# Second half of the node counts moved from the build into pass 0 of a two-network GNN kernel

## The chip, the cores and the metric

The kernel runs on one core of one Trainium2 chip. The metric is the device time of one execution in microseconds (us), as the median of several runs; less is faster. The kernel before takes 1076.45 us (median of 3 runs, 1075.31 to 1078.13). A core has four engines that compute (PE, the matrix engine; DVE, the vector engine; ACT, the scalar engine; POOL, the general one) and SP, which here only issues DMA transfers and waits. POOL issues DMA transfers too. Engines wait for each other and for transfers by semaphores: an instruction waits until a counter has reached a value.

## The reference: what is computed

A graph of 6250 nodes (64 features each) and 200000 directed edges (src to dst, sorted by dst, 16 attributes each) goes through two small networks, each followed by a residual sum and a layer norm:

```
def sage_conv(x, src, dst, W_l, b_l, W_r, n_nodes):        # first network, two of these
    msg = x[src]
    agg = segment_sum(msg, dst)
    cnt = segment_sum(ones, dst)
    mean = agg / maximum(cnt, 1.0)
    return mean @ W_l.T + b_l + x @ W_r.T

def mp_layer(x, src_f, dst_f, ea_f, W, b):                 # second network, three of these
    m = concatenate([x[dst_f], x[src_f], ea_f], axis=1) @ W.T + b
    return relu(segment_sum(m, dst_f))                     # with a self loop on each node

x = layernorm(x + conv2(relu(conv1(x))))
x = layernorm(x + mp3(bn_relu(mp2(bn_relu(mp1(x))))))
```

The change concerns `cnt` of the first network: how many edges end in each node, and 1 / max(cnt, 1), by which the sum over a node's neighbours is divided.

## The kernel before, in words

The kernel never gathers messages. In a first part, `build`, it makes the dense matrix of edge multiplicities (6272 by 6272, one byte each, `adj` in DRAM) in 25 stages of 256 columns. Each of the five aggregations (passes 0 to 4) is then a matrix product of the node features (`Xop`) with `adj`, in 13 blocks of 512 columns (`NB`), 49 matmuls of 128 rows to a block.

In the build DVE makes one-hot tables and unpacks finished stages (`unpack`, L806 and L807), PE multiplies tables (L929), ACT evacuates. POOL writes each unpacked stage to `adj` (`keep`, L631). Because all of pass 0 needs only the input features, its products are made in the build: of the first 21 stages by `product` (L904), stored in DRAM as `s0`, and of the last four by `remaining` (L314), which leaves its result in PSUM. Stages 21, 22 and 23 are multiplied at the end of the build and stage 24 behind the barrier, at the start of pass 0. Two staging buffers (`Xop1` and a part of `Aring`) take turns: stage 24 is unpacked into the one that stage 22 was in, so its unpack waits on `s_fin` for the product of stage 22.

The build also sums the edge attributes of each node (`ea_sum`, 33 rows in DRAM; row 32 is the count). The counts become factors in two pieces: nodes 0 to 3583 (`EARLY`) within the build, and nodes 3584 to 6271 (the later nodes) at its end. For a piece SP loads row 32 of `ea_sum` as 16 partitions (L599), DVE runs `counts` (sum for a check, max with 1, reciprocal, scale: L1090, L1092, L1094, L1096), and SP stores the result in `rc_d` (L604). From `rc_d` SP broadcasts the factors to 128 partitions (`reciprocals`, L299), in three pieces: blocks 0 and 1, blocks 2 to 5, blocks 6 to 12. Only the third needs the later nodes' counts of `rc_d`. `products` (L292) brings `s0` back in four pieces, and `given` (L305) brings the transposed input features `in_xT` in two, the second of 1312 KB after the last unpack, since it overwrites what the unpack reads (`F`).

What SP issues, it issues in the order of its program, and all of it goes through one queue. A barrier over all engines stands between the build and pass 0 (L379), and another between passes (L1162).

Pass 0, for each block b: DVE multiplies the stored product by the factors (`sums`, L1832, two instructions), PE applies two weight matrices (`post`, L1659 and L1660), ACT the relu (L2011), PE the next layer's weights (`post2`, L1687), DVE updates the residual and splits the result into a high and a low half (`rest`, L1901, L1891, L1893, L1894). DVE's program runs by turns: turn i holds `sums(i-1)` and then `rest(i-3)`. PE's turn i holds `post(i-1)` and then `post2(i-2)`. SP meanwhile waits for the later nodes' store and for the last writes of `adj` to land, and then loads the third piece of factors, the factors of pass 1, and the first six stages of `adj` (`Ares`, L1540). Passes 1 to 4 are dominated by the products (L1460).

Of the kernel before, what the change touches and what calls it, by code (L numbers as in the profile page):

```python
# [9 lines left out]
NP = NT * 128  # L10
SW = 256
NST = 25
# [106 lines left out]
NH = -(-NS // HS)  # L119
# [112 lines left out]
EARLY = 3584  # L232
# [38 lines left out]
def spread(m, name, cnt, a, b):  # L271

    x = (m["ea_sum"][32, :] if name == "ea_sum" else m[name])[a:b]
    return x.rearrange("(p c) -> p c", p=16), cnt[:, 0:(b - a) // 16]
# [10 lines left out]
def products(sp, m, i):  # L285

    b0, b1 = SUMS[i]
    stored = [st for st in range(2 * b0, min(NST, 2 * b1)) if RANK[st] < EARLIER]
    for z in range(2):
        sp.wait_ge(m["s_so"][z], 16 * max(RANK[st] // 2 + 1 for st in stored if RANK[st] % 2 == z))  # L290
    for c0, c1 in joined(stored):
        sp.dma_start(raw_sums(m)[:, c0:c1], m["s0"][:, c0:c1]).then_inc(m["s_sr"][i], 16)  # L292
# [84 lines left out]
def build(nc, ins, m):  # L377
    ctx = ExitStack()
    with ctx:  # L379
# [67 lines left out]
        ja = within(3, [128, RW], f16)  # L447

        late = G[0:16, 0, 0:(NP - EARLY) // 16].bitcast(f32)
        packed = m["F"][:].bitcast(u16).rearrange("p (r c) -> p r c", r=4)  # L450
        stage = [m["Xop"][1][:].rearrange("p a b -> p (a b)").bitcast(u16), m["Aring"][:, 1, 1, :].bitcast(u16)]

# [39 lines left out]
        s_st, s_eo, s_so = m["s_st"], m["s_eo"], m["s_so"]  # L492
# [25 lines left out]
        def unpacked_after(h):  # L518

            return [f for f in range(NST) if (stage_end[f] == h - 1 if h < NH else stage_end[f] >= h - 1)]  # L520
# [21 lines left out]
        def _(sp):  # L542
# [24 lines left out]
            for c in range(NCH):  # L567
# [6 lines left out]
                if c == NCH - 2:  # L574
                    for i in range(2):
                        sp.wait_ge(s_eo[i], 16 * (EARLY // SW // 2))
                    there, here = spread(m, "ea_sum", cnt, 0, EARLY)
# [7 lines left out]
            there, here = spread(m, "rc_d", cnt, 0, EARLY)  # L585
# [7 lines left out]
            given(sp, ins, m, 0)  # L593
            reciprocals(sp, m, 1)
            products(sp, m, 1)
            for i in range(2):
                sp.wait_ge(s_eo[i], 16 * (13 - i))
            there, here = spread(m, "ea_sum", late, EARLY, NP)
            sp.dma_start(here, there).then_inc(m["s_cl"], 16)  # L599
            products(sp, m, 2)  # L600
            products(sp, m, 3)
            sp.wait_ge(m["s_cr"], 8)
            there, here = spread(m, "rc_d", late, EARLY, NP)
            sp.dma_start(there, here).then_inc(m["s_cd"], 16)  # L604
            sp.wait_ge(s_un, NST)
            given(sp, ins, m, 1)

# [86 lines left out]
        def _(v):  # L694
# [170 lines left out]
            for i in range(3):  # L865
                nc.vector.tensor_scalar(m["ws"][i][:], m["ws"][i][:], m["scl"][:, 0:1], None, ALU.mult)
                nc.vector.tensor_scalar(m["wc"][i][:], m["wc"][i][:], m["scl"][0:97, 1:2], None, ALU.mult)
            for f in unpacked_after(NH)[:-1]:
                unpack(f)
            v.wait_ge(m["s_cl"], 32)  # L870
            counts(nc, v, late, m["csum"][:, 1, :], m["s_cr"], 4)
            unpack(NST - 1)

        @block.tensor
        def _(pe):
# [212 lines left out]
def counts(nc, v, cnt, total, s_cr, made):  # L1088

    nc.vector.tensor_reduce(total, cnt.rearrange("p (c i) -> p i c", i=4), AX.X, ALU.add).then_inc(s_cr, 1)  # L1090
    v.wait_ge(s_cr, made + 1)
    nc.vector.tensor_single_scalar(cnt, cnt, 1.0, ALU.max).then_inc(s_cr, 1)  # L1092
    v.wait_ge(s_cr, made + 2)
    nc.vector.reciprocal(cnt, cnt).then_inc(s_cr, 1)  # L1094
    v.wait_ge(s_cr, made + 3)
    nc.vector.tensor_single_scalar(cnt, cnt, 1 / CS, ALU.mult).then_inc(s_cr, 1)  # L1096
# [368 lines left out]
def propagate(nc, ins, m, t, p, sem, out, past, block, closing=None):  # L1465
# [30 lines left out]
    fused = p == 0 and not slow  # L1496
# [11 lines left out]
    @block.sync  # L1508
    def _(sp):
        def factors(b):  # L1510

            n, c = blk(b), b * 512
            if b >= 2:
                sp.wait_ge(s_r, b - 1)
            src = (m["rc_d"] if p <= 1 else m["ea_sum"][32, :])[c:c + n].rearrange("(o n) -> o n", o=1)
            rows = 128 if p <= 1 else 64
            sp.dma_start(rc[0:rows, b % 2, 0:n], src.broadcast_to([rows, n])).then_inc(s_c[b % 2], 16)

        def next_factors(b):

            src = m["rc_d"][b * 512:(b + 1) * 512].rearrange("(o n) -> o n", o=1)
            sp.dma_start(rc[:, b], src.broadcast_to([128, 512])).then_inc(t["s_cf"][b], 16)

        def late_factors():
            sp.wait_ge(t["s_cr"], 4)
            there, here = spread(m, "rc_d", t["cnt"], 0, NP)
            sp.dma_start(there, here).then_inc(t["s_cd"], 16)
            sp.wait_ge(t["s_cd"], 16)

        if fused:  # L1530
            sp.wait_ge(m["s_cd"], 32)
            for i in range(2):
                sp.wait_ge(m["s_st"][i], 16 * (13 - i))
            sp.wait_ge(m["s_fin"], NST - 1 - EARLIER)
            reciprocals(sp, m, 2)
            for b in range(2):
                next_factors(b)
            for b in range(RB):
                for h in range(2):
                    sp.dma_start(t["Ares"][:, b, h, :], m["adj"][2 * b + h]).then_inc(m["s_res"][b], 16)  # L1540
            sp.dma_start(F[64:97, 0:NP], m["ea_sum"][:, 0:NP]).then_inc(t["s_ea"], 16)
            sp.wait_ge(s_r, NB)
            for b in range(2):
                for h in range(2):
                    sp.dma_start(t["Aring"][:, b, h, :],
                                 m["adj"][2 * (RB + b) + h]).then_inc(t["s_ar"][b][h], 16)
            return
        if p == 0:
            late_factors()
        if p != 1 or slow:  # L1550
            factors(0)
            factors(1)
        for b in range(NB):
            nxt = b + 2 if b + 2 < NB else b + 2 - (NB - RB)
            if b >= RB and not slow and not (b + 2 >= NB and p == 4):
                i = ring(b)[0]
                sp.wait_ge(t["s_mm"], mm0 + b + 1)
                if (p, b) in CHECKED:
                    sp.wait_ge(t["s_ck"], CHECKED.index((p, b)) + 1)
                for h in range(2 if nxt < NB - 1 else 1):  # L1560
                    n = stage_width(2 * nxt + h)
                    sp.dma_start(t["Aring"][:, i, h, 0:NT * n], m["adj"][2 * nxt + h, :, 0:NT * n]).then_inc(
                        t["s_ar"][i][h], 16)
            if b + 2 < NB:
                factors(b + 2)
        if closing:
            closing(sp, lambda part, engine: part.run_sync(engine), lambda: None)
# [177 lines left out]
    def _(v):  # L1745
# [184 lines left out]
        if p == 0 and slow:  # L1930
            late_counts()

        lag = {1: 1, 4: 3}.get(p, 2)

        def turn(i):

            if (p, i) == (2, NB - 1):
                check(i)
            if 1 <= i <= NB:
                sums(i - 1)  # L1940
            if i >= lag + 1:
                rest(i - lag - 1)
            if (p, i) == (3, 2):
                check(1)
            if i < NB and (p, i) not in ((2, NB - 1), (3, 1)):
                check(i)
            if p == 4 and not slow:
                tell(i)
# [229 lines left out]
```

## Time and profile before

| what | before |
|---|---|
| median of 3 runs | 1076.45 us (1075.31 to 1078.13) |
| the profiled execution | 1076.73 us, of which the span of its instructions is 1074.9 us |
| granted TensorE clock, mean | 0.949 of full speed |
| PE busy | 925.9 us (86%) |
| DVE busy | 689.6 us (64%) |
| end of the build's last matmul, start of the next one | 398.81 us, 407.26 us |

The span counts from the first instruction to the last; the execution's own time lies 1.8 us above it. A row of the timeline gives the start, the time taken, engine, line, operation, output and inputs, how many instructions are merged in the row (x2), and in brackets how long the engine had been idle before and what ended that. Rows of SPq and POOL's DMA rows show the issue of a transfer, not the transfer. Matmul ends are modelled, so rows of PE overlap a little.

### The profile page before, as it was taken

What the parts mean: (1) busy time and instruction counts of PE and PEld (TensorE: products, weight loads), DVE (VectorE), ACT (ScalarE), POOL (GpSimd) and SP (SyncE); (2) the same over time, 40 slices, a digit from 0 to 9 for tenths busy, and PEclk for the clock granted to TensorE, in tenths of its full rate; (3) what the DMA queues carried; (4) which work ended last, traced back from release to release, by engine and by line L of the source; (5) the groups of instructions that cost most, each with busy time, mean ns of one, the idle gap of its engine ahead of it and who ended that gap; (6) DMA issues with size and microseconds to landing.
All of it is one profiled execution on the core that took longest, in us unless ns stands there. A gap on an engine that the chain in (4) does not pass through costs nothing. (4 is left out here: it accounts for less than half of the span.)

```text
span 1074.9 us, 19163 instructions
## 1 busy us (share of the span) xinstructions
PE 925.9 (86%) x7566; PEld 566.6 (53%) x7566; DVE 689.6 (64%) x1289; ACT 404.6 (38%) x846; POOL 129.8 (12%) x148
## 2 busy tenths in 40 slices
PE   0348877979687878999999999997999997999995
PEld 0347776868687864545555544444444444444443
DVE  5997989999999954623433656655385456332334
ACT  1684788889787821100000010104311022411113
POOL 4121323244322220000000000000000000000001
PEclk9868998989899998999999999998999998999998
DMA  6425546756576497953775607776018775037771
GB/s 176 82 77 204 189 134 203 254 143 211 176 213 185 110 339 255 370 230 140 295 311 204 250 16 291 309 271 251 21 32 320 295 280 240 11 106 296 269 282 31
DMA packets 64873, 217.02 MB, mean 202 GB/s; under 512 B 28955, under 2 KB 42860, under 8 KB 51236
## 3 DMA queue, kind: packets, MB, share of 16 engines
q1 hardware_dynamic: 55444, 164.26, 42.9%
q0 software_dynamic: 9328, 51.44, 13.7%
q8 instruction: 62, 1.02, 0.4%
q14 instruction: 39, 0.31, 0.1%
HBM read 170.43 MB, written 45.22 MB: 201 GB/s over the span
## 5 line engine op out<-in xcount | busy, mean ns | idle before, releaser
L1460 PE MATMUL PM<-Aring,Xop 128*128 128x512 fp8e4 (+1 forms) x1960 | 396.7, 363 | 2.0 <-issue 2.0
L1460 PEld LDWEIGHTS PM<-Aring,Xop 128*128 128x128 f16 x1960 | 182.2, 98 | 213.8 <-issue 11.0
L1460 PE MATMUL PM<-Ares,Xop 128*128 128x512 fp8e4 x588 | 137.1, 388 | 2.9 <-ACT Xop L2072 1.4
L929 PE MATMUL PM<-Aring 128*128 128x104 fp8e4 (+3 forms) x1616 | 96.8, 219 | 38.1 <-ACT F L998 38.1
L1834 DVE TENSOR_SCALAR S<-PM 128x256 f32<-128x256 f32 x72 | 30.5, 424 | 152.9 <-PE PM L1460 64.6
L2023 ACT ACTIVATE F<-PH,bag 64x512 f32<-64x512 f32 (+1 forms) x39 | 25.7, 660 | 260.5 <-PE PH L1677 259.9
L929 PEld LDWEIGHTS PM<-Aring 128*128 128x128 fp8e4 x1616 | 87.6, 105 | 41.4 <-ACT F L998 40.2
L1460 PEld LDWEIGHTS PM<-Ares,Xop 128*128 128x128 f16 x588 | 56.2, 100 | 70.5 <-issue 7.7
L1590 POOL DMA_DIRECT2D out<-hT x12 | 9.0, 754 | 654.0 <-DVE hT L1791 654.0
L782 DVE TENSOR_TENSOR Aring<-Ares 128x4096 uint16<-128x4096 uint16 x31 | 70.8, 2283 | 5.5 <-PE PW L929 5.2
L998 ACT ACTIVATE F<-PM 128x392 uint16<-128x392 f32 x147 | 67.2, 515 | 7.3 <-PE PM L929 5.7
L1864 DVE TENSOR_TENSOR hT<-hT,Aring 128x1536 uint16<-128x1536 uint16 (+2 forms) x71 | 67.6, 952 | 2.3
L789 DVE TENSOR_TENSOR Aring<-Ares 128x1144 uint16<-128x1144 uint16 (+22 forms) x139 | 67.2, 546 | 0.0
L904 PE MATMUL PX<-Aring,Xop 128*128 128x256 fp8e4 x490 | 58.5, 282 | 5.4 <-ACT Ares L1017 5.4
L904 PE MATMUL PX<-Xop 128*128 128x256 fp8e4 (+1 forms) x539 | 59.1, 271 | 0.6 <-ACT Ares L1017 0.6
L1832 DVE TENSOR_TENSOR S<-PM,rc 128x256 f32<-128x256 f32 (+1 forms) x25 | 9.3, 413 | 76.5 <-PE PM L1460 74.2
L904 PEld LDWEIGHTS PX<-Aring,Xop 128*128 128x128 f16 x490 | 49.4, 102 | 12.6 <-issue 5.5
L929 PE MATMUL PW<-Aring 128*128 128x104 fp8e4 (+3 forms) x535 | 34.6, 211 | 24.9 <-ACT F L998 22.2
L904 PEld LDWEIGHTS PX<-Xop 128*128 128x128 f16 x539 | 51.1, 99 | 6.8 <-issue 0.8
L2015 ACT ACTIVATE st_<-st_ 128x4 f32<-128x4 f32 (+1 forms) x13 | 2.7, 205 | 131.6 <-DVE st_ L1765 131.6
L882 PE MATMUL PT<-ident,Ares 128*128 128x128 f32 x32 | 8.7, 366 | 42.0 <-ACT Ares L960 42.0
L942 PE MATMUL PA<-Ares,ea 128*128 128x64 f16 (+1 forms) x1000 | 38.9, 202 | 3.6 <-ACT odd L1009 3.6
(169 smaller groups left out, 1256.0 us busy)
## 6 DMA issues: line engine op xcount, KB each, us to landing
Aring<-adj SPq DMA_DIRECT2D x72, 1568.0 KB, 9.8
adj<-Aring POOLq DMA_DIRECT2D x12, 1568.0 KB, 6.7
adj<-Xop POOLq DMA_DIRECT2D x12, 1568.0 KB
Ares<-adj SPq DMA_DIRECT2D x6, 1568.0 KB, 19.8
rc<-ea_sum SPq DMA_DIRECT2D x36, 128.0 KB, 6.7
Aring<-adj SPq DMA_DIRECT2D x4, 784.0 KB, 4.5
rc<-rc_d SPq DMA_DIRECT2D x12, 256.0 KB, 9.6
eaf<-in_erow SPq DMA_DIRECT2D x60, 51.0 KB, 2.1
```

The source lines that it names most:

```text
L782: nc.vector.tensor_tensor(lo[:, h % 2].rearrange("p s (i j e) -> p s i j e", i=8, e=2), At[:, t % 2, at:at + HS].rearrange("p s i (o e) -> ...
L789: last = nc.vector.tensor_tensor(key[:, o:o + 26 * n].rearrange("p (q v e) -> p q v e", v=26, e=2), Dv[:, t % 2, d, i:i + n].rearrange("p ...
L904: last = nc.tensor.matmul(PX[:, 0:n], m["Xop"][0][:, h, :], of[:, h, :], start=h == 0, stop=h == NT - 1)
L929: last = nc.tensor.matmul(PW[begun % RING][:, c:c + 52 * (z - y)].rearrange("p (d v b) -> p d v b", d=z - y, b=2), lo[:, h % 2, i, :].bitc ...
L942: last = nc.tensor.matmul(PA[st % 2][:, o:o + 2 * PD].rearrange("p (d e) -> p d e", e=2)[:, :, e:f], ea_flat[:, c % 2, j * GW:j * GW + 128 ...
L998: nc.scalar.activation(to, PW[g % RING][:, 0:416].rearrange("p (q h) -> p h q", h=52)[:, 0:NT], ACT.Copy, scale=32.0).then_inc(s_wev, 1)
L1460: last = nc.tensor.matmul(o, x[:, h, :], rhs, start=h == 0, stop=h == NT - 1)
L1590: g.dma_start(out[b * 512:(b + 1) * 512, :].rearrange("(j q) f -> q j f", q=128), fin[:, b % 4]).then_inc(s_o[b % 4], 16)
L1832: last = nc.vector.tensor_tensor(part, of, natural(by), ALU.mult)
L1834: own(nc.vector.tensor_single_scalar(part, of, 1 / CS, ALU.mult))
L1864: own(nc.vector.tensor_tensor(to[:, 0:h1 - h0], to[:, 0:h1 - h0], of[:, h0:h1], ALU.add))
L2023: nc.scalar.activation(F[0:64, c:c + w], PH[b // 2 % 2][64 * (b % 2):64 * (b % 2) + 64, 0:w], ACT.Relu, bias=t["bag"][:, 4 + conv:5 + conv ...
```

## The change

The later nodes' counts leave the build. Their load, their store and DVE's four instructions are now in pass 0, behind the barrier: SP issues the load first thing there, DVE works on it between the sums of block 1 and those of block 2, and SP then stores the factors, before everything else that SP did in pass 0. In the build the last stage's unpack stands directly behind the one before.

```
@@ build, SP
             products(sp, m, 1)
-            for i in range(2):
-                sp.wait_ge(s_eo[i], 16 * (13 - i))
-            there, here = spread(m, "ea_sum", late, EARLY, NP)
-            sp.dma_start(here, there).then_inc(m["s_cl"], 16)
             products(sp, m, 2)
             products(sp, m, 3)
-            sp.wait_ge(m["s_cr"], 8)
-            there, here = spread(m, "rc_d", late, EARLY, NP)
-            sp.dma_start(there, here).then_inc(m["s_cd"], 16)
             sp.wait_ge(s_un, NST)
             given(sp, ins, m, 1)
@@ build, DVE
-            for f in unpacked_after(NH)[:-1]:
+            for f in unpacked_after(NH):
                 unpack(f)
-            v.wait_ge(m["s_cl"], 32)
-            counts(nc, v, late, m["csum"][:, 1, :], m["s_cr"], 4)
-            unpack(NST - 1)
@@ propagate, SP
         if fused:
+            for i in range(2):
+                sp.wait_ge(m["s_eo"][i], 16 * (13 - i))
+            there, here = spread(m, "ea_sum", m["late"], EARLY, NP)
+            sp.dma_start(here, there).then_inc(m["s_cl"], 16)
+            sp.wait_ge(m["s_cr"], 8)
+            there, here = spread(m, "rc_d", m["late"], EARLY, NP)
+            sp.dma_start(there, here).then_inc(m["s_cd"], 16)
             sp.wait_ge(m["s_cd"], 32)
@@ propagate, DVE
+        def last_counts():
+            v.wait_ge(m["s_cl"], 32)
+            counts(nc, v, m["late"], m["csum"][:, 1, :], m["s_cr"], 4)
+
         def turn(i):
             ...
             if 1 <= i <= NB:
                 sums(i - 1)
+            if fused and i == 2:
+                last_counts()
             if i >= lag + 1:
                 rest(i - lag - 1)
```

`m["late"]` is the same piece of SBUF as before, handed from the build to pass 0.

DVE around the barrier, before (the unpacks of stages 23 and 24 into `Aring` and `Xop1`, between them the counts, then the sums of blocks 0, 1 and 2):

```order
L806 TENSOR_SCALAR Aring<-F 128x2x49x32 [waits s_fin,s_st1,s_wev]
L807 TENSOR_SCALAR Aring<-F 128x2x49x32
L1090 TENSOR_REDUCE csum<-Ares 16x4 [waits s_e_cl]
L1092 TENSOR_SCALAR Ares<-Ares 16x168 [waits s_e_cr]
L1094 RECIPROCAL Ares<-Ares 16x168 [waits s_e_cr]
L1096 TENSOR_SCALAR Ares<-Ares 16x168 [waits s_e_cr]
L806 TENSOR_SCALAR Xop1<-F 128x2x49x32 [waits s_fin,s_st0,s_wev]
L807 TENSOR_SCALAR Xop1<-F 128x2x49x32
L379 UNCONDITIONAL_BRANCH
...
L1832 TENSOR_TENSOR S<-Aring 128x256 [waits s_rb0,s_sr0]
...
L1832 TENSOR_TENSOR S<-Aring 128x256 [waits q0_S,s_rb0,s_sr0]
...
L1832 TENSOR_TENSOR S<-PM2,Aring 128x256 [waits q0_S,q0_h,s_fin,s_rb1]
```

And of the changed kernel (its lines stand a few lower, L800 for L806, L1830 for L1832):

```order
L800 TENSOR_SCALAR Aring<-F 128x2x49x32 [waits s_fin,s_st1,s_wev]
L801 TENSOR_SCALAR Aring<-F 128x2x49x32
L800 TENSOR_SCALAR Xop1<-F 128x2x49x32 [waits s_fin,s_st0,s_wev]
L801 TENSOR_SCALAR Xop1<-F 128x2x49x32
L379 UNCONDITIONAL_BRANCH
...
L1830 TENSOR_TENSOR S<-Aring 128x256 [waits s_rb0,s_sr0]
...
L1830 TENSOR_TENSOR S<-Aring 128x256 [waits q0_S,s_rb0,s_sr0]
...
L1081 TENSOR_REDUCE csum<-Ares 16x4 [waits q0_S,s_e_cl]
L1083 TENSOR_SCALAR Ares<-Ares 16x168 [waits s_e_cr]
L1085 RECIPROCAL Ares<-Ares 16x168 [waits s_e_cr]
L1087 TENSOR_SCALAR Ares<-Ares 16x168 [waits s_e_cr]
L1830 TENSOR_TENSOR S<-PM2,Aring 128x256 [waits q0_h,s_fin,s_rb1]
```

The wait for the counts' load (`s_e_cl`) moved from ahead of the last unpack to ahead of block 2's sums.

SP's queue before, from the second piece of `in_xT` back to the first piece of factors (`s0` the stored products, `ea_sum` the counts):

```order
L299 DMA Aring<-rc_d 128x1024 [waits s_e_cd]
L305 DMA F<-in_xT 64x1024 [waits s_un]
L299 DMA Aring<-rc_d 128x2048
L292 DMA Aring<-s0 128x1024 [waits s_so1,s_so0]
L599 DMA Ares<-ea_sum 16x168 [waits s_eo1,s_eo0]
L292 DMA Aring<-s0 128x2560 [waits s_so1,s_so0]
L292 DMA Aring<-s0 128x640 [waits s_so1,s_so0]
L604 DMA rc_d<-Ares 16x168 [waits s_e_cr]
L305 DMA F<-in_xT 64x5248 [waits s_un]
L379 UNCONDITIONAL_BRANCH
...
L299 DMA Aring<-rc_d 128x3200 [waits s_st1,s_fin,s_st0,s_e_cd]
```

And of the changed kernel, from the load of the products for blocks 2 to 5 on:

```order
L292 DMA Aring<-s0 128x1024 [waits s_so1,s_so0]
L292 DMA Aring<-s0 128x2560 [waits s_so1,s_so0]
L292 DMA Aring<-s0 128x640 [waits s_so1,s_so0]
L305 DMA F<-in_xT 64x5248 [waits s_un]
L379 UNCONDITIONAL_BRANCH
L1419 UNCONDITIONAL_BRANCH [waits barrier_Pool_Activation_PE_DVE_SP_release]
L1525 DMA Ares<-ea_sum 16x168 [waits s_eo1,s_eo0]
L1528 DMA rc_d<-Ares 16x168 [waits s_e_cr]
L299 DMA Aring<-rc_d 128x3200 [waits s_st1,s_fin,s_st0,s_e_cd]
```

The load of the counts now stands behind three more transfers of SP, the 64x5248 of `in_xT` last. PE's and POOL's programs are the same in both kernels.

## Rows read from the trace of the kernel before

**Rows 1.** The page: busy time of the engines over the span.
```profile
PE 925.9 (86%) x7566; PEld 566.6 (53%) x7566; DVE 689.6 (64%) x1289; ACT 404.6 (38%) x846; POOL 129.8 (12%) x148
```

**Rows 2.** Timeline of PE around the barrier.
```profile
387.95 5.51 PE L314 MATMUL PM<-Xop 128*128 128x256 fp8e4 x49
393.30 5.51 PE L314 MATMUL PM<-Aring,Xop 128*128 128x256 fp8e4 x49
407.26 0.77 PE L1440 MATMUL PB<-scl,wc 33*64 33x1 f32 x6 [8.45 <-PEq L379]
407.96 8.12 PE L314 MATMUL PM<-Xop 128*128 128x256 fp8e4 x49
415.92 1.02 PE L1659 MATMUL PH<-S,wl 128*128 128x512 f32 x2
...
421.03 1.02 PE L1659 MATMUL PH<-S,wl 128*128 128x512 f32 x2
...
424.03 1.02 PE L1659 MATMUL PH<-S,wl 128*128 128x512 f32 x2
```

**Rows 3.** Timeline of DVE around the barrier.
```profile
402.02 0.43 DVE L1090 TENSOR_REDUCE csum<-Ares 16x4 f32<-16x168 f32 x1 [11.91 <-DMA Ares<-ea_sum]
...
403.98 0.23 DVE L1096 TENSOR_SCALAR Ares<-Ares 16x168 f32<-16x168 f32 x1
404.15 0.96 DVE L806 TENSOR_SCALAR Xop<-F 128x3136 uint16<-128x3136 uint16 x1
405.03 0.96 DVE L807 TENSOR_SCALAR Xop<-F 128x3136 uint16<-128x3136 uint16 x1
407.34 0.76 DVE L1832 TENSOR_TENSOR S<-Aring 128x256 f32<-128x256 f32 x2 [1.35 <-PEq L379]
...
418.14 0.76 DVE L1832 TENSOR_TENSOR S<-PM,Aring 128x256 f32<-128x256 f32 x2 [9.06 <-PE PH L1660]
```

**Rows 4.** Timeline of SP: when its transfers are issued.
```profile
389.97 1.54 SPq L292 DMA_DIRECT2D Aring<-s  x2
404.25 0.32 SPq L604 DMA_DIRECT2D rc_d<-Ares  x1
406.02 0.48 SPq L305 DMA_DIRECT2D F<-in_xT  x1
418.68 0.34 SPq L299 DMA_DIRECT2D Aring<-rc_d  x1
```

**Rows 5.** Transfers issued from 380 to 425 us: size, time from issue to landing.
```profile
Aring<-rc_d SPq DMA_DIRECT2D x1, 1600.0 KB, 6.2
...
adj<-Xop POOLq DMA_DIRECT2D x1, 1568.0 KB
F<-in_xT SPq DMA_DIRECT2D x1, 1312.0 KB, 9.7
...
Aring<-s SPq DMA_DIRECT2D x1, 320.0 KB, 15.2
...
Ares<-ea_sum SPq DMA_DIRECT2D x1, 10.5 KB, 12.6
rc_d<-Ares SPq DMA_DIRECT2D x1, 10.5 KB, 1.6
```

**Rows 6.** Timeline of POOL: the last write of a stage is issued.
```profile
406.28 0.54 POOL L631 DMA_DIRECT2D adj<-Xop  x1 [15.32 <-DVE Xop L807]
```

**Rows 7.** Windows: us, busy by engine, PEclk, DMA share, GB/s.
```profile
395.00:400.00 5.00, 3.81 (x35) 3.17 (x33) 0.00 (x0) 0.00 (x0) 0.00 (x0) 1.00 0.99 417
400.00:405.00 5.00, 0.00 (x0) 0.00 (x0) 2.88 (x5) 0.00 (x0) 0.00 (x0) 0.81 0.81 338
405.00:410.00 5.00, 2.74 (x16) 2.19 (x17) 2.51 (x6) 0.15 (x1) 0.54 (x1) 0.50 0.69 138
410.00:415.00 5.00, 5.00 (x33) 3.83 (x32) 0.00 (x0) 0.00 (x0) 0.00 (x0) 0.67 0.87 235
```

**Rows 8.** Waits of SP: row from the list of its longest waits.
```profile
SPq L1534 <- DMA adj<-Xop: 11.4, 1, 11.4
```

**Rows 9.** Timeline of PE at the next barrier.
```profile
460.67 2.97 PE L1460 MATMUL PM<-Ares,Xop 128*128 128x512 fp8e4 x13
463.96 10.74 PE L1460 MATMUL PM<-Ares,Xop 128*128 128x512 fp8e4 x49 [0.32 <-PEq L1162]
```

**Rows 10.** The first six stages: durations of the issues, and their landings.
```profile
L1540 SPq DMA_DIRECT2D Ares<-adj x6: 443/451/635, 420.0 to 422.6; - x6
...
DMA to landing us min/median/max: 11.9/19.8/29.6
```

**Rows 11.** The early counts' load, alone in the queue.
```profile
Ares<-ea_sum SPq DMA_DIRECT2D x1, 14.0 KB, 1.7
```

**Rows 12.** Timeline of DVE: the sums of block 6.
```profile
431.71 0.76 DVE L1832 TENSOR_TENSOR S<-Aring 128x256 f32<-128x256 f32 x2
```

More of the change, by code:

```diff
@@ L449, in build @@
         late = G[0:16, 0, 0:(NP - EARLY) // 16].bitcast(f32)
+        m["late"] = late
         packed = m["F"][:].bitcast(u16).rearrange("p (r c) -> p r c", r=4)
```

## The prediction

> **What bounds the kernel now.** I read the page first: PE is busy for 86% of the span [rows 1], so the time is PE's, plus the holes in its work. Then the timeline of PE around the barrier: the product of stage 23 ends at 393.30 + 5.51 = 398.81 us, and PE does nothing until 407.26 [rows 2]. The timeline of DVE shows why. DVE stands 11.91 us before L1090 for the load of the later nodes' counts, which lands at 402.0, works on the counts until 404.2, unpacks stage 24 until 405.99, and only then lets the barrier go [rows 3]. POOL's write of that stage is issued last, at 406.28 for some 0.5 us [rows 6]. So this wait is on the path, for 8.45 us of PE's idleness.
>
> After it PE pays once more: the 49 matmuls of stage 24 take 8.12 us where the same 49 took 5.51 before the hole [rows 2]. The windows show the granted clock at 0.81, 0.50 and 0.67 from 400 to 415 us, that is at 1.2 GHz for most of that stretch, behind a stretch in which PE had nothing to do [rows 7]. That is 2.61 us for coming back from an idle PE.
>
> From 415.92 on pass 0 is a chain on PE alone, 3.00 us a block (421.03 to 424.03) [rows 2]; DVE waits for PE in it, 9.06 us before block 2's sums [rows 3].
>
> **The change, part by part.** The order of the program says what moves; the times come from the rows.
>
> *The last unpack.* It loses its wait for the counts and keeps that for the product of stage 22, which ends at 387.95 + 5.51 = 393.46 [rows 2]. The two instructions take from 404.15 to 405.99, 1.84 us [rows 3], and now end at about 395.5. No one waits for that, since PE works to 398.81.
>
> *The barrier.* PE is last at it. At the next barrier, where PE is last too, 460.67 + 2.97 = 463.64 and 463.96 leave 0.32 us [rows 9]. So pass 0 begins on PE at 399.1 and not at 407.26: 8.1 us earlier. PE hardly stops and should keep its clock, so L1440 and the product of stage 24 end at 399.1 + 0.7 + 5.5 = 405.3, and not at 415.9. PE's next work up to block 2's post (two posts, one post2) takes 421.03 - 415.92 = 5.1 us [rows 2], to 410.4. Were nothing else late, that would be the gain: 421.0 - 410.4 = 10.6 us.
>
> *What is late next: the counts' load.* DVE meets it right behind the sums of block 1, at 399.2 + 2 = 401. Behind the waiting L1081 stand the four counts' instructions, block 2's sums, and with them PE's post of block 2. SP can issue the load only behind the barrier, at about 399.3. It then stands in SP's queue behind two products of 1280 and 320 KB and, new, behind the 1312 KB of `in_xT`, which the early unpack lets SP issue at 395.6 and not at 406.02 [rows 4, 5]. That a small load waits for the ones ahead shows in the trace: these 10.5 KB took 12.6 us, where 14 KB in an empty queue took 1.7 [rows 5, 11].
>
> So when does it land? The last of the products landed at about 390.5 + 15.2 = 405.7 [rows 4, 5] and that stays. The 1312 KB took 9.7 us from issue to landing [rows 5], of which I take off the 1.7 us of a small load [rows 11], since it is now issued long before its turn: 8.0 us, 413.7. Beside it there is a second new competitor, POOL's write of stage 24, 1568 KB, issued at about 395.8 and not 406.28.
>
> Bounds. Below: the DMA engines carry everything at the 417 GB/s of the fullest window [rows 7]. The two transfers together are 2.95 MB, 7.1 us; the window from 400 to 405 leaves (417 - 338) x 5 us = 0.4 MB of room, 0.9 us; so 405.0 + 7.1 - 0.9 = about 411. Above: `in_xT` keeps its own 8.0 us and the write's 1.6 MB at 417 GB/s go wholly ahead of it, 3.9 us: 417.6. I take the middle, 414.4, because `in_xT` alone moved at only 138 GB/s in its first window, so it has room beside the write, but shares the engines with it [rows 7].
>
> *The counts.* From the landing to the instruction behind them: 404.15 - 402.02 = 2.13 us [rows 3]. Block 2's sums begin at 416.5, take 0.76 [rows 3], and PE's post of block 2 starts at about 417.4, against 421.03: 3.6 us gained. PE has then been idle from 410.4 to 417.4, 7.0 us, close to the 8.45 that cost it its clock before. I charge the 2.61 us once more, now on the small matmuls of pass 0. (Between nothing, if the clock holds, and that.)
>
> *SP's rest.* The store of the factors waits for the counts: 416.6, landed 1.6 later [rows 5] at 418.2; then the third piece of factors at 418.4, where before SP waited until 418.68 for the write of stage 24 [rows 4, 8], which now lands sooner. So this and the stages of `adj` behind it keep their place in time. The third piece lands 6.2 us later [rows 5], at 424.6, and block 6, which needs it, comes at 431.71 before [rows 12] and at about 430.7 now. The first two stages of `adj` land by about 436, the third and fourth by 443, the last by 452.2 [rows 10]; the next pass begins at 463.96 [rows 9]. Nothing there is short, and this whole chain keeps its distance however late the load lands, since both hang on it.
>
> *The sum.* 3.6 gained less 2.6 for the clock is 1.0 us. All later passes run on PE and should move by that. Against its own execution (1076.73, of which 1074.9 is the span) that gives 1075.7; the median of the runs shown is 0.3 lower, so I forecast 1075.4.
>
> The Trainium skill has a figure that speaks on the load's price. Its page "DMA: Bandwidth & Descriptors", section "Anatomy of one DMA — SWDGE (gpsimd) path", puts the fixed cost of a transfer at about 2 us. An estimate by that figure alone has the load landed at 401.3, and the whole 10.6 us gained. The trace agrees for an empty queue only (1.7 us) and denies it for this one (12.6 us).
>
> **The rivals.**
>
> *A. As forecast:* load at 412.5 to 416.5, with the clock's price; 1 us faster, 1073.5 to 1077.5. Chance 0.55.
>
> *B. The queue drains at the full rate.* Load at 411, post of block 2 at 414.0: 7.0 gained, 2.6 paid if PE's idle 3.6 us still cost the clock: 4.4 faster, 1072.0. If the clock holds, 1069.4. For it: 0.99 busy and 417 GB/s from 395 to 400. Against it: 138 and 235 GB/s while exactly these two transfers ran, 405 to 415 [rows 7]. Chance 0.18.
>
> *C. Slower: the counts' load waits behind everything.* POOL's write goes first, then the products, then `in_xT` at its own pace: load at 417.6. The post of block 2 comes at 420.6, 0.4 us gained, the idle PE pays 2.6: 2.2 slower, 1078.7. It decides from a landing of 415.4 on, where 3.6 - 1.0 is used up. If it lands past 418.7, the loss exceeds 0.3%. The 12.6 us of this load in the old place speak for it; that less is left in the queue when it is issued speaks against. Chance 0.22.
>
> The same page of the Trainium skill, section "Queues, rings and completion order", lets an engine drain a whole packet of descriptors from one queue before it turns to the next. Taken alone that would be this case C, as POOL's write of a stage could be one such packet per engine; no row here separates it from a finer interleaving.
>
> *D. The load lands by itself within about 2 us of 399.3.* Then DVE is never late, and PE's own 10.6 us are gained: 1065.8. Against it stands the 12.6. Chance 0.05.
>
> **How the numbers follow.** What a measurement of this kernel can tell from no change is about 0.3%, 3.2 us: faster is below 1073.2, slower above 1079.7. D, nearly all of B, and a little of A's early end are faster: 0.22. C's late half and what I have not seen are slower: 0.13. The rest, 0.65, is no difference. The range from 1072.0 to 1079.0 holds A and most of B and C.
>
> **What would show it right or wrong.** The first matmul of pass 0 near 399.1; the product of stage 24 in 5.5 us at full clock; `in_xT` issued near 395.6; DVE before L1081 idle for 11 to 16 us with the counts' load as the releaser; the issue of the load near 399.3 and its landing 13 to 17 us later; PE idle for 5 to 8 us before block 2's post, and the granted clock low behind that and not behind the barrier. It is wrong if DVE does not wait for the load (D), if the clock holds through PE's hole (then 2.6 us more gained), or if something behind pass 0 waits that did not.

## The result and the profile after

| | before | changed |
|---|---|---|
| median, runs beside each other | 1076.68 us (20 runs, 1073.80 to 1079.38) | 1079.69 us (20 runs, 1076.79 to 1085.25) |
| ratio to before, 95% interval | | 1.0031 (1.0020 to 1.0043) |
| again, in a later set | 1077.62 us (15 runs) | 1079.03 us (11 runs), 1.0024 (1.0014 to 1.0034) |
| the profiled execution | 1076.73 us | 1076.79 us; in the later set 1078.53 us |

The change makes the kernel slower: at the median by 3.0 us in the first set and 1.4 us in the later one, and in both sets the interval of the ratio lies above 1. I had forecast 1 us faster, 1075.4, in a range from 1072.0 to 1079.0.

The first profile of the changed kernel is of its fastest execution of 20, so its total says nothing of the loss. Its rows around the barrier do, and the second profile has the same ones. Everything up to the build's last matmul is the same in all kernels here but for a drift of some tenths to 2.6 us between executions, so from here on I count from the end of that matmul (E): 398.81 us before, 394.49 + 5.51 = 400.00 in the changed kernel.

The timeline of PE, changed kernel: answers to [rows 2].

```profile
394.49 5.51 PE L314 MATMUL PM<-Aring,Xop 128*128 128x256 fp8e4 x49
400.45 0.48 PE L1431 MATMUL PB<-scl,wc 33*64 33x1 f32 x6 [0.44 <-PEq L379]
400.86 5.52 PE L314 MATMUL PM<-Xop 128*128 128x256 fp8e4 x49
...
410.33 1.16 PE L1685 MATMUL PG<-w,hT 128*128 128x128 f32 x8
421.70 2.07 PE L1657 MATMUL PH<-S,wl 128*128 128x512 f32 x2 [10.21 <-DVE S L1830]
423.70 2.07 PE L1658 MATMUL PH<-F,wr 64*128 64x512 f32 x2
425.71 2.07 PE L1685 MATMUL PG<-w,hT 128*128 128x128 f32 x8
```

The hole at the barrier is gone: 8.45 us have become 0.44, and the product of stage 24 takes 5.52 us and not 8.12. PE is through the first post2 at E + 11.5. Then it stands 10.21 us, and block 2's post begins at E + 21.7; before it began at 421.03, E + 22.2. So 0.5 us is left of 10.7.

The timeline of DVE, changed kernel: answers to [rows 3].

```profile
418.79 0.43 DVE L1081 TENSOR_REDUCE csum<-Ares 16x4 f32<-16x168 f32 x1 [16.52 <-DMA Ares<-ea_sum]
...
420.91 0.74 DVE L1830 TENSOR_TENSOR S<-PM,Aring 128x256 f32<-128x256 f32 x2
```

DVE waits for the counts' load, now 16.52 us and not 11.91, and with PE behind it. The transfers, changed kernel (KB, us from issue to landing): answers to [rows 5].

```profile
adj<-Xop POOLq DMA_DIRECT2D x1, 1568.0 KB, 12.1
F<-in_xT SPq DMA_DIRECT2D x1, 1312.0 KB, 21.9
...
Aring<-s SPq DMA_DIRECT2D x1, 320.0 KB, 21.8
...
Ares<-ea_sum SPq DMA_DIRECT2D x1, 10.5 KB, 18.3
rc_d<-Ares SPq DMA_DIRECT2D x1, 10.5 KB, 1.4
```

And the issues (SP, changed kernel): `in_xT` at 396.68, the load at 400.46.

```profile
396.68 0.48 SPq L305 DMA_DIRECT2D F<-in_xT  x1
400.46 0.33 SPq L1525 DMA_DIRECT2D Ares<-ea_sum  x1
```

So `in_xT` lands at 396.68 + 21.9 = 418.6 and the load at 400.46 + 18.3 = 418.8, right behind it. In all five profiles in which the load stands behind `in_xT` in SP's queue (these two of the changed kernel, kept_warm, kept_warm_40 and given_by_home below) it lands within 0.3 us of it. The products that stand ahead land later too: the 320 KB took 21.8 us and not 15.2, which is to 412.9.

Windows of the changed kernel (us, busy by engine, PEclk, DMA share, GB/s), the coarse ones as in [rows 7], then finer ones.

```profile
400.00:405.00 5.00, 4.56 (x45) 4.14 (x45) 1.52 (x4) 0.15 (x1) 0.00 (x0) 1.00 1.00 426
405.00:410.00 5.00, 5.00 (x21) 2.17 (x19) 0.00 (x0) 0.69 (x1) 0.00 (x0) 1.00 1.12 397
410.00:415.00 5.00, 1.49 (x9) 0.97 (x8) 0.00 (x0) 0.69 (x1) 0.00 (x0) 0.96 0.85 175
415.00:420.00 5.00, 0.00 (x0) 0.00 (x0) 1.15 (x3) 0.00 (x0) 0.00 (x0) 0.50 0.06 14
420.00:425.00 5.00, 3.30 (x4) 1.00 (x4) 3.78 (x10) 0.00 (x0) 0.00 (x0) 0.50 0.37 115
425.00:430.00 5.00, 5.00 (x14) 2.59 (x13) 2.11 (x6) 0.69 (x1) 0.00 (x0) 0.68 0.74 264
```
```profile
409.00:414.00 5.00, 2.49 (x11) 1.26 (x10) 0.00 (x0) 0.71 (x2) 0.00 (x0) 1.00 1.06 219
412.00:414.00 2.00, 0.00 (x0) 0.00 (x0) 0.00 (x0) 0.00 (x0) 0.00 (x0) 1.00 1.21 252
414.00:416.00 2.00, 0.00 (x0) 0.00 (x0) 0.00 (x0) 0.00 (x0) 0.00 (x0) 0.65 0.13 26
416.00:418.00 2.00, 0.00 (x0) 0.00 (x0) 0.00 (x0) 0.00 (x0) 0.00 (x0) 0.50 0.05 11
```

The reader is to see three things. The low clock has moved: 0.50 now stands at 415 to 425, behind PE's new idle stretch. From 409 to 414, with POOL's write landed at 409.1 and only SP's queue at work, 219 GB/s move, where 426 moved from 400 to 405. And from 414 on hardly anything begins (26, then 11 GB/s) while the load still hasn't landed.

A window counts a packet where it begins, and the 64 packets of `in_xT`, 20992 bytes each, take 1.62 us each. So the trace's records of single packets are more exact here. Sixteen are under way at a time until 414, nine at 415.0, three at 415.5, and a last one until 418.0. The bulk is through at 415.5; the last 3.3 us wait for a few leftovers.

The trace also records when each of the 16 parts of a transfer lands. Of the load fourteen parts had landed by 416.5, the fifteenth came at 418.2 and the last at 418.8; of `in_xT` fourteen by 416.3 and the last at 418.6. So what everyone waits for in the end is one or two parts of sixteen, 2.3 us behind the rest. The second profile has the same (fourteen by 415.0, the last at 417.3).

Where the time went is clearest in three distances from E, in each profile.

| kernel | block 2's post | pass 1 begins | from post to pass 1 |
|---|---|---|---|
| before | E + 22.2 | E + 65.2 | 42.9 |
| changed | E + 21.7 | E + 67.8 | 46.1 |
| changed, second profile | E + 21.3 | E + 67.6 | 46.3 |

Pass 1 begins 2.4 to 2.7 us late. Block 2's post is 0.5 to 0.9 us early, and 3.2 to 3.4 us are lost behind it, at the low clock. In the first profile the loss is given back behind pass 1: pass 1 begins 3.9 us later than before on the profile's own count, and behind pass 2, at about 750 us, it is still 3.9; 30 us on it is 2.7, and the rest goes in smaller pieces up to the end. The first of these steps is at a place where the clock falls and rises by itself, around the 4.7 us in which PE stands between two passes. Before (first fence) the two windows at the low clock are 0.50 and 0.54; in the changed kernel (second) 0.50 and 0.91.

```profile
745.00:750.00 5.00, 2.66 (x12) 1.47 (x13) 1.98 (x7) 3.99 (x7) 0.00 (x0) 0.50 1.02 437
750.00:755.00 5.00, 5.00 (x16) 1.91 (x15) 0.85 (x2) 1.49 (x3) 0.00 (x0) 0.54 0.73 307
```
```profile
750.00:755.00 5.00, 3.79 (x14) 1.89 (x15) 1.61 (x4) 3.97 (x7) 0.00 (x0) 0.50 1.01 427
755.00:760.00 5.00, 5.00 (x26) 2.13 (x25) 1.70 (x4) 1.44 (x3) 0.00 (x0) 0.91 0.47 201
```

Both kernels have that idle stretch. The second profile of the changed kernel gains 1.1 us there too, so it isn't what sets the two profiles apart, and no run here shows what makes the low stretch shorter.

### The profile page after: what moved, and what is told of

It is laid out like the page before. It is cut to its first block and busy times, and to the rows that moved or that the text cites. A ratio compares the mean times of both kernels' runs of the same rounds, so it can differ in the third digit from the quotient of the medians.

```text
span 1075.0 us, 19163 instructions
## 1 busy us (share of the span) xinstructions
PE 924.6 (86%) x7566; PEld 565.1 (53%) x7566; DVE 689.5 (64%) x1289; ACT 403.9 (38%) x846; POOL 128.5 (12%) x148
## 5 line engine op out<-in xcount | busy, mean ns | idle before, releaser
L1832 DVE TENSOR_SCALAR S<-PM 128x256 f32<-128x256 f32 x72 | 30.5, 424 | 152.2 <-PE PM L1451 64.3
L1862 DVE TENSOR_TENSOR hT<-hT,Aring 128x1536 uint16<-128x1536 uint16 (+2 forms) x71 | 67.6, 952 | 2.3
L1830 DVE TENSOR_TENSOR S<-PM,rc 128x256 f32<-128x256 f32 (+1 forms) x25 | 9.4, 414 | 76.5 <-PE PM L1451 74.2
L920 PE MATMUL PW<-Aring 128*128 128x104 fp8e4 (+3 forms) x535 | 34.3, 210 | 24.6 <-ACT F L989 22.2
```

The costliest lines, as they stand in the source:

```text
L920: last = nc.tensor.matmul(PW[begun % RING][:, c:c + 52 * (z - y)].rearrange("p (d v b) -> p d v b", d=z - y, b=2), lo[:, h % 2, i, :].bitc ...
L1830: last = nc.vector.tensor_tensor(part, of, natural(by), ALU.mult)
L1832: own(nc.vector.tensor_single_scalar(part, of, 1 / CS, ALU.mult))
L1862: own(nc.vector.tensor_tensor(to[:, 0:h1 - h0], to[:, 0:h1 - h0], of[:, h0:h1], ALU.add))
```

## The experiments

Eleven kernels ran. The table has their medians, the ratio to the runs of before beside them, and the distances; what was edited and expected follows.

| kernel | median us | ratio (95%) | block 2's post | pass 1 begins |
|---|---|---|---|---|
| load_in_build | 1075.69 | 0.9999 (0.9983 to 1.0014) | E + 18.9 | E + 65.2 |
| given_by_home | 1078.63 | 1.0026 (1.0017 to 1.0035) | E + 22.1 | E + 71.3 |
| both | 1071.13 | 0.9947 (0.9926 to 0.9969) | E + 12.4 | E + 60.5 |
| kept_warm | 1081.54 | 1.0048 (1.0035 to 1.0061) | E + 26.9 | E + 70.0 |
| kept_warm_40 | 1077.94 | 1.0007 (0.9993 to 1.0020) | E + 22.1 | E + 65.2 |
| unpack_alone | 1078.33 | 1.0008 (0.9996 to 1.0019) | E + 22.6 | E + 65.6 |
| other_queue | 1071.91 | 0.9953 (0.9937 to 0.9970) | E + 16.0 | E + 58.9 |
| other_queue_by_home | 1073.10 | 0.9967 (0.9955 to 0.9979) | E + 18.7 | E + 61.6 |
| build_other_queue | 1072.62 | 0.9950 (0.9936 to 0.9963) | E + 17.0 | E + 59.9 |
| pass0_other_queue | 1067.31 | 0.9899 (0.9884 to 0.9914) | E + 11.3 | E + 56.4 |
| changed_again | 1079.03 | 1.0024 (1.0014 to 1.0034) | E + 21.3 | E + 67.6 |

**The load back at its old place.** The theory was that the counts' load and `in_xT` bind equally; the rival, that the load alone is late.

```
@@ build, SP
             products(sp, m, 1)
+            (the two waits on s_eo, and the load, as before the change)
@@ propagate, SP
-            (the same lines)
```

> The changed kernel, but SP issues the later nodes' counts' load at its old place in the build; DVE's counts and the store stay in pass 0. Theory 1 (the counts' load and the second piece of in_xT land together, 418.75 and 418.6 us, so in_xT holds block 2's post on PE just as long): the load lands by about 403, DVE is done with the counts by 405, and PE now waits for in_xT; the post of block 2 starts near 418.8 and not at 421.7, PE's clock still falls, and the time is about 3 us below the changed kernel's 1079.7, near 1076.7. Theory 2 (only the counts' load is late): block 2's post starts near 411.5, the clock holds, 10 + 3 us less: 1066 to 1068.

The load landed by 406.6 (some 3 us later than expected, in 15.2 us), DVE was through the sums of block 2 by 410, and PE still stood. The rows of DVE, of SP's issue, of the transfer and of PE:

```profile
409.21 0.76 DVE L1830 TENSOR_TENSOR S<-PM,Aring 128x256 f32<-128x256 f32 x2 [0.42 <-PE PH L1658]
```
```profile
397.46 0.48 SPq L305 DMA_DIRECT2D F<-in_xT  x1
```
```profile
F<-in_xT SPq DMA_DIRECT2D x1, 1312.0 KB, 22.2
```
```profile
419.72 2.04 PE L1657 MATMUL PH<-S,wl 128*128 128x512 f32 x2 [7.45 <-issue]
```

`in_xT` landed at 397.46 + 22.2 = 419.7, and at 419.72 block 2's post began. The row names no releaser, but in the program this post waits for three things, the sums, its piece of `in_xT` and ACT's relu of block 0, and the sums and the relu were there by 410. So theory 1 holds: with the load out of the way PE waits for `in_xT`, at E + 18.9. The change of place gave 4.0 us against the changed kernel's first set, and put the time back where it was before the change.

**`in_xT` cut at block 6.** The columns of `F` for blocks 0 to 5 are free at the first piece's wait already.

```
-GIVEN = [(0, 2), (2, NB)]
+GIVEN = [(0, 6), (6, NB)]
```

> The changed kernel, but in_xT is cut at block 6 and not at block 2: the part for blocks 0 to 5 goes into columns of F that are already free at the first piece's wait, so 1.5 MB moves from two pieces of 256 and 1312 KB to 768 and 800 KB, and what stands ahead of the counts' load behind the early unpack is 800 KB and not 1312. The total in SP's queue is the same. Theory (the load waits for all that is ahead): it lands only 1 to 3 us earlier, since the queue's bytes are the same and only in_xT's own slow pace starts earlier; 1077 to 1079. Rival (the 1312 KB alone set the landing): 500 KB less at 168 KB per us is 3 us, and more if PE's hole then no longer costs the clock: 1073 to 1077.

The load landed at 417.9, E + 19.2, where it was E + 18.8 in the changed kernel. The cut alone moves nothing: the same bytes stand ahead. Neither size that I gave was right; the time is in the forecast range because nothing changed, which is luck. This profile shows the worst case of the clock: PE idle for 10.64 us, and then 0.50 to past 430.

```profile
420.00:425.00 5.00, 4.18 (x5) 1.18 (x6) 2.93 (x9) 0.07 (x1) 0.00 (x0) 0.50 0.54 184
425.00:430.00 5.00, 5.00 (x12) 2.53 (x12) 2.17 (x6) 0.62 (x1) 0.00 (x0) 0.50 0.72 276
430.00:435.00 5.00, 5.00 (x13) 2.50 (x12) 2.17 (x6) 0.69 (x1) 0.00 (x0) 0.62 1.01 431
```

From post to pass 1 it is 49.2 us here, where it was 42.9 before and 46.1 in the changed kernel: after a similar idle stretch the clock came back later.

**Both edits.**

> Both edits: the counts' load at its old place in the build, and in_xT cut at block 6. By theory 1 nothing of block 2 waits any more for a transfer behind the barrier: PE's post of block 2 starts near 411.5, the clock stays at full, 10.2 us of waiting and some 3 us of low clock go: 1066 to 1069. If something else of block 2 is late (the write of stage 24, which the first residual sum waits for, lands at 409) a part of it remains: above 1070.

Block 2's post starts at E + 12.4. The two edits give 8.6 us together against the changed kernel, where one alone gave 4.0 and the other 1.1 (no more than the noise). It missed 1066 to 1069 for a wait that I hadn't listed: the store of the factors stood in the queue behind `in_xT` for 7.3 us, the third piece of factors went out at 418.14, and block 6 waited for it. DVE's row, which costs PE a stop of 1.77 us, and the window behind it, in which the clock is low:

```profile
rc_d<-Ares SPq DMA_DIRECT2D x1, 10.5 KB, 7.3
```
```profile
424.70 0.76 DVE L1830 TENSOR_TENSOR S<-Aring 128x256 f32<-128x256 f32 x2 [2.38 <-DMA Aring<-rc_d]
```
```profile
425.00:430.00 5.00, 4.48 (x6) 1.47 (x7) 2.63 (x8) 0.37 (x1) 0.00 (x0) 0.52 0.95 396
```

**PE kept busy in the idle stretch.**

```
@@ propagate, PE
+            if fused and i == 3:
+                for _ in range(70):                       # 40 in kept_warm_40
+                    nc.tensor.matmul(PB[:, 128:256], m["ident"][:, 0:64], m["w2"][:], start=True, stop=True)
             if 1 <= i <= NB:
                 post(i - 1)
```

> The changed kernel, with 70 matmuls of 128 by 128 float32 (a constant by a constant, result not used) on PE between the first post2 and block 2's post, where PE stands idle for 10.2 us; they take about 9.2 us. Theory (the idle stretch costs the clock, and the low clock costs pass 0 3.2 us: block 6's post is 3.9 us later than before, block 2's only 0.7): the granted clock stays 1.0 until pass 2's end, block 2's post starts at the same place, and the time is 3 us below the changed kernel's, 1076.7. Rival (the low clock costs nothing, as pass 0 then waits for DVE and ACT): no change, 1079.7.

Here I was wrong about the length: each matmul is done in two, so 70 took 15.50 us and ended at 426.05, 6 us behind the sums. So it is slower, and tells little by its time. From its post to pass 1 it is 43.0 us, as before the change. Hence a second one, with 40.

> The changed kernel with 40 constant matmuls on PE in its idle stretch of 10.2 us, not 70: 70 took 15.5 us (each is done in two) and ended 4.5 us after the counts were ready; 40 take 8.9 us and end before. Theory: the granted clock stays 1.0 and block 6's post comes 3 us sooner against block 2's; 3 us below the changed kernel's 1079.7, 1076.7. Rival (the low clock costs nothing here): 1079.7.

```profile
411.60 8.95 PE L1726 MATMUL PB<-w,ident 128*64 128x128 f32 x80
422.30 1.13 PE L1657 MATMUL PH<-S,wl 128*128 128x512 f32 x2 [1.75 <-DVE S L1833]
```
```profile
415.00:420.00 5.00, 5.00 (x48) 5.00 (x47) 0.60 (x2) 0.00 (x0) 0.00 (x0) 1.00 0.07 15
420.00:425.00 5.00, 3.25 (x15) 1.49 (x13) 4.34 (x11) 0.49 (x1) 0.00 (x0) 1.00 0.18 64
```

The clock stays at 1.00, block 2's post comes at the same distance as before (E + 22.1), and pass 1 begins at E + 65.2, as before the change. The median falls by 1.8 us against the first set, the ratio from 1.0031 to 1.0007. So the low clock is the whole of the loss in the profile's distances. By the times it is probably most of it: the interval of this kernel's ratio ends at 1.0020, where that of the changed kernel's first set begins, and overlaps that of its later set; of the 3 us that I had expected, 1.8 came.

**One part of the change alone: the last unpack ahead of the counts.**

```
-            for f in unpacked_after(NH)[:-1]:
+            for f in unpacked_after(NH):
                 unpack(f)
             v.wait_ge(m["s_cl"], 32)
             counts(nc, v, late, m["csum"][:, 1, :], m["s_cr"], 4)
-            unpack(NST - 1)
```

> The kernel before with one part of the change alone: in the build, the last stage's unpack stands ahead of the wait for the later nodes' counts; load, counts and store stay in the build. The load lands at 402.0, the counts are done at 404.2, and the barrier goes at 404.7 and not at 407.3; in_xT, which SP issues behind the store, goes at 404.5 and lands by about 414 to 416. PE has idled 6 us, its clock falls, and block 2's post comes at 404.7 + 0.7 + 8.1 + 5.1 = 418.6 and not at 421.0. Theory: 2.4 us faster than before, 1074. Rival (POOL's write of stage 24 beside in_xT delays it past 420): as before or slower.

The theory fell. The load took 15.4 us and landed at 404.8, not 402.0; PE's hole at the barrier grew from 8.45 to 10.11 us, and no time was gained.

```profile
395.50 0.54 POOL L631 DMA_DIRECT2D adj<-Xop  x1 [4.79 <-DVE Xop L807]
```
```profile
404.82 0.43 DVE L1089 TENSOR_REDUCE csum<-Ares 16x4 f32<-16x168 f32 x1 [9.62 <-DMA Ares<-ea_sum]
```
```profile
Ares<-ea_sum SPq DMA_DIRECT2D x1, 10.5 KB, 15.4
```

What differs ahead of that load is the write of stage 24, which POOL issued at 395.50 and not at 406.28. So an early write of 1568 KB delays what SP has in its queue, by some 3 us, in one profile of each. Fourteen of the load's sixteen parts came only 1.6 us later than before, counted from E; the rest is again the last part, 1.9 us behind them.

**The load in a queue of its own.** ACT issues it, the rest is the kernel before.

```
@@ build, SP
-            (the two waits on s_eo, and the load)
@@ build, ACT, at the end
+            act.wait_ge(s_sti, TS + PT)
+            (the two waits on s_eo)
+            act.dma_start(here, there).then_inc(m["s_cl"], 16)
```

> The kernel before, but the load of the later nodes' counts is issued by ACT, in a queue of its own, and not by SP behind three transfers. Everything else stands where it stood, the counts in the build too. Theory (the queue ahead, not the load, took the 12.6 us): the load lands within 2 to 5 us, DVE does the counts while it would wait for PE's product of stage 22 anyway, the last unpack ends near 396, the barrier goes when PE is done, near 399.5, and the hole of 8.45 us is gone. But in_xT is then issued early too, behind the products, and lands near 418, and block 2's post waits for it as in the changed kernel with the load in the build: no more than 2 to 3 us faster than before, 1074 to 1076. Rival (in_xT doesn't bind): 1066.

```profile
Ares<-ea_sum ACTq DMA_DIRECT2D x1, 10.5 KB, 8.2
F<-in_xT SPq DMA_DIRECT2D x1, 1312.0 KB, 13.1
```
```profile
402.82 0.48 PE L1441 MATMUL PB<-scl,wc 33*64 33x1 f32 x6 [3.43 <-PEq L379]
```

8.2 us and not 2 to 5: a queue of its own takes 4.4 us off the 12.6, not all. The DMA engines themselves were busy (a mean share of 0.99 from 389 to 397.6). The counts were done late enough for a hole of 3.43 us, so `in_xT` was issued at 401.57, landed at 414.7, and didn't bind: block 2's post came at 415.36. It is faster than I expected for that reason, 1071.9.

> The kernel of other_queue with in_xT cut at block 6, so that blocks 2 to 5 wait for no late transfer. Theory: block 2's post at about 410.5, the clock holds at least to block 6; block 6 needs the third piece of factors, which SP issues once the write of stage 24 has landed (near 409), behind the second part of in_xT: landed by 422 to 425, a wait of up to 4 us where block 6 could go at 422. 1067 to 1071, no slower than the 1071.1 of the kernel with both edits. Rival: the store of the factors and the third piece stand behind in_xT just as there: 1071.

No better than without the cut (1073.1): the hole at the barrier was 4.62 us here, and took the clock for longer. The theory's 410.5 forgot that hole.

> The kernel of other_queue_by_home with the last unpack ahead of the wait for the counts; counts and store in the build. The write of stage 24 is then issued near 396 beside the load, which lands near 398 to 400; barrier near 401 to 403, in_xT's second part issued at that time behind the store. PE idles 2 to 4 us. Theory: block 2's post at 412 to 414, 1068 to 1071. Rival (the early write of stage 24 delays the counts' load, as in unpack_alone, where it took 15.4 us against 12.6): load past 402, and no faster than 1073.

The counts' load took 7.3 us and landed near 401.7, and the barrier still went late, 4.44 us of hole: between theory and rival.

```profile
405.58 0.48 PE L1440 MATMUL PB<-scl,wc 33*64 33x1 f32 x6 [4.44 <-PEq L379]
```

**The change with its transfers mended.** Counts in pass 0, as in the changed kernel; load (in the build) and store (in pass 0) through ACT's queue; `in_xT` cut at block 6.

```
@@ propagate, ACT, ahead of the first relu
+        if fused:
+            act.wait_ge(m["s_cr"], 8)
+            there, here = spread(m, "rc_d", m["late"], EARLY, NP)
+            act.dma_start(there, here).then_inc(m["s_cd"], 16)
```

> The changed kernel with the counts in pass 0 as they are, but their load (issued in the build) and their store (in pass 0) go through ACT's queue, and in_xT is cut at block 6. Theory: the load lands near 398, the counts are made at 401, block 2's post starts at 410.5 behind the first post2 with no wait, the store lands by 408, the clock holds; block 6 waits at most 2 us for the third piece of factors. Some 10 us faster than before at block 2: 1066 to 1069, and faster than the kernel with both edits (1071.1), where the load took 17.2 us and the store 7.3. Rival (the DMA engines, not the queue, are the limit): 1071.

The time is as expected, 1067.31 us, 1.0% faster than before (0.9884 to 0.9914), though the load landed at 400.2 and not 398, and the store at 410.9 and not 408. DVE does not wait for the load any more, and PE goes on at once:

```profile
402.08 0.43 DVE L1086 TENSOR_REDUCE csum<-Ares 16x4 f32<-16x168 f32 x1
```
```profile
410.00 1.16 PE L1683 MATMUL PG<-w,hT 128*128 128x128 f32 x8
410.99 1.02 PE L1655 MATMUL PH<-S,wl 128*128 128x512 f32 x2
...
425.00 1.13 PE L1655 MATMUL PH<-S,wl 128*128 128x512 f32 x2 [1.84 <-DVE S L1828]
```

What is left is a stop of 1.84 us at block 6, for the third piece of factors, which took 13.2 us behind the rest of `in_xT`. Here the clock stays at 1.00 behind it, where it fell behind the 1.77 us of the kernel with both edits:

```profile
425.00:430.00 5.00, 5.00 (x16) 2.08 (x16) 3.80 (x11) 0.69 (x1) 0.00 (x0) 1.00 1.00 429
```

Its neighbour is build_other_queue, with the same early unpack, load and cut, but the counts in the build: 1072.62 us. So once the transfers are out of the way, the counts in pass 0 (with their store through ACT) are worth 5.3 us. The idea of the change was sound; its load stood in the wrong place.

**The changed kernel again.**

> The changed kernel once more, for a second profile: the first one's execution took 1076.8 us, the shortest of 20, so it doesn't show the 3 us by which the median rose. Expected: the same order at the barrier (load of the counts landing 18 to 20 us after its issue, PE idle for 9 to 12 us before block 2's post, low clock until some 6 us behind it), pass 1 beginning 3 to 5 us later than before against the build's end, and a median of 1079 to 1080. Rival (the median came from something before the barrier or in the later passes): those waits as in the first profile, and the time lost elsewhere.

```profile
417.29 0.43 DVE L1081 TENSOR_REDUCE csum<-Ares 16x4 f32<-16x168 f32 x1 [16.11 <-DMA Ares<-ea_sum]
```
```profile
420.20 2.08 PE L1657 MATMUL PH<-S,wl 128*128 128x512 f32 x2 [9.78 <-DVE S L1830]
```

The median, 1079.03, PE's idle stretch and the low clock are as expected. Pass 1 began 2.4 us later than before and not 3 to 5, and the load landed 17.9 us after its issue, just under my 18. So the waits are the same in both profiles, and the rival fell.

## Why the prediction was wrong

*The last unpack and the barrier.* Right: 395.6, 0.44 us of hole instead of 8.45, the product of stage 24 at full clock in 5.52 us.

*The landing of the counts' load.* This is the term that failed. I put it between 411 and 417.6 and took the middle, 414.4. It came at 418.8, which is 417.6 counted from the same end of the build (417.2 in the second profile): the upper end, my case C to the tenth. I argued for the middle with the rate at which `in_xT` moved alone. But I bounded the landing by bytes over the mean rate of all DMA engines, and a transfer lands with its last piece. The bulk was through at 415.5, which is 414.3 on the same count, about when my middle had the landing, and the wait ended 3.3 us behind that. Of the 3.2 us by which I missed, 2.3 are the last two of the load's sixteen parts. Why those parts lag is not shown.

My reading of `in_xT`'s pace was wrong too. I took 138 GB/s in the window from 405 to 410 to mean that it leaves room beside it. But its first packet began at 407.3, and from 408.5 to 412 sixteen of its packets were under way at every time, as many as in the fullest windows, which is 16 x 20992 bytes in 1.62 us, 207 GB/s. POOL's write, issued at 406.28, began to move only at 412. So `in_xT` is slow and leaves no room, and my lower bound, which lets it move at 417 GB/s, wasn't to be had.

That case C is right to the tenth is in part luck, since two of its terms were wrong and cancel. I had the last of the products land at 405.7, "and that stays"; it landed at 412.9, 6.0 us later on the same count, where case C has them through at 405.7 + 3.9 = 409.6. And `in_xT` landed 5.7 us behind them, not 8.0.

At the load's old place, unpack_alone and other_queue show two things that it waits for: the early write of stage 24 costs about 3 us, the queue of SP 4.4. At its place in the changed kernel neither was taken away by itself, so how its 18.3 us divide stays open.

*What it is worth.* From the landing to block 2's post the sum held (3.0 us; measured 421.70 - 418.8 = 2.9). So block 2's post gained 0.5 us where I had 3.6; for case C I had written 0.4.

*The clock.* The place was right, PE's idle stretch in pass 0, and kept_warm_40 shows it: without the low clock pass 1 begins as early as before. I charged 2.6 us, from the product of stage 24; PE stood for 10.2 and 9.8 us and not 7, and it was 3.2 and 3.4 us in the two profiles and 6.3 in given_by_home. The step that was wrong is to take one measured return as the price of all.

*The rest of SP's chain.* It kept its distance, as I said; the third piece of factors went out at 422.38, some 3 us later than I had it, as the load was, and block 6 didn't wait.

*Rival D was not there to be had.* I gave 10.6 us if the load came at once, and counted `in_xT` only as something ahead of the load. Block 2's post needs it by itself, and load_in_build shows PE waiting for it with the counts long done. I read the wait that the change moved and not the wait of the same instruction for another transfer of the same queue, `in_xT`, which stands right ahead of the load.

*The sum.* 0.5 to 0.9 gained and 3.2 to 3.4 lost gives 2.4 to 2.7 slower at the start of pass 1 in the profiles, and 3.0 (first set) and 1.4 (second) in the medians. Case C, 2.2 slower at a chance of 0.22, is what happened, if in part by luck. Why single executions of the changed kernel spread further, up to 1085, the profiles do not settle. The 6.3 us that given_by_home lost at the low clock, 3 more than the changed kernel's profiles, would be enough for half of it; this was only argued.

## What to carry to other kernels

A wait that is moved behind a barrier is paid by whoever works there: look at who is queued behind it, and at what its transfer is queued behind once everything ahead of it is issued earlier. Bound a landing by the slowest piece of the transfers ahead, not by bytes over the mean rate, and then ask of each instruction that becomes free which other transfer it needs. A small, urgent transfer deserves a queue without bulk in it. Three things together turned the change from 3 us slower to 10 us faster than before: the load issued early, in the build; the cut that took `in_xT` off the path; and a queue of their own for load and store. The first two alone (the kernel with both edits) brought it to 5 us faster than before, a ratio of 0.9947; the queue gave the rest, to 0.9899.

## What the runs showed of the hardware

- A load of 10.5 KB took 12.6 to 18.7 us on SP's queue behind its large transfers, and 7.3 to 8.5 us in a queue where nothing stood ahead, while the DMA engines were busy with others. 14 KB in a quiet stretch took 1.7 us [rows 11].
- In the changed kernel the last of a transfer's 16 parts landed 2.3 us behind the fourteenth, for the counts' load and for the 1312 KB ahead of it, with three packets under way at 415.5 us and one until 418.0, where sixteen were before. In the kernel before it was 0.4 us for the same load.
- The 1312 KB of `in_xT`, into 64 partitions, moved at 207 GB/s with sixteen packets under way all the time, so that nothing ran beside it (kernel before, 408.5 to 412 us). From 400 to 405 us in the changed kernel POOL's write and SP's products moved 426 GB/s together.
- After PE had stood for 7 to 11 us its clock was at 0.50 for the next matmuls, and the return cost pass 0 between 3.2 and 6.3 us in four profiles (both of the changed kernel, load_in_build, given_by_home). Constant matmuls in the idle stretch kept it at 1.00. A stop of 1.8 us was followed by a clock of 0.52 in one kernel (both) and of 1.00 in two others (pass0_other_queue, kept_warm_40).
